# Third place for the decays of a selective scan, in SBUF, and another order in which ScalarE makes them

## What is computed

```python
xp = x @ x_proj_w.T                          # 64 ranks, 16 B columns, 16 C columns
delta = softplus(d_rank @ dt_proj_w.T + dt_proj_b)
deltaA = exp(delta[..., None] * A)           # the decays: rows x channels x 16 states
deltaB_u = delta[..., None] * Bm * x
h = deltaA_t * h + deltaB_u_t                # step by step along the 1024 rows
y = (h * C).sum(states) + x * D
```

## Time and profile before

| what | value |
|---|---|
| median of 3 executions | 4587.7 us (4587.43 to 4588.58) |
| profiled execution, its own time | 4590.48 us |
| its span, first to last instruction | 4588.0 us |
| VectorE (DVE) busy over the span | 3844.8 us, 84% |
| GpSimd (POOL) busy | 3435.0 us, 75% |
| TensorE (PE) busy | 2972.6 us, 65% |
| ScalarE (ACT) busy | 2824.3 us, 62% |
| mean granted TensorE clock | 0.691 of full speed |

### The profile page before, as it was taken

The page is one execution under the profiler, slowest core; times in us unless marked ns, Lnnn a source line. Parts: engine busy times, 40 slices in busy tenths (PEclk is TensorE's granted clock), DMA queues, the critical chain, the costliest instruction groups (busy, mean ns, idle before and its releaser), DMA issues. The chain is left out here.

```text
span 4588.0 us, 60367 instructions
## 1 busy us (share of the span) xinstructions
PE 2972.6 (65%) x17062; PEld 1351.1 (29%) x17062; DVE 3844.8 (84%) x3098; ACT 2824.3 (62%) x4359; POOL 3435.0 (75%) x1748
## 2 busy tenths in 40 slices
PE   3656565656575656566665656565654289999997
PEld 1222222222222222222222222222222145555553
DVE  3999999999999999999999999999998645555542
ACT  5777777777767777777777777777665223232221
POOL 3999999999999999999999999999997100000010
PEclk7667575656565656666575657565655599999998
DMA  4454546364645455454545463646443300000000
GB/s 104 97 135 116 151 105 163 82 167 93 161 102 143 114 136 144 106 140 111 139 115 148 103 159 88 166 93 162 101 126 74 147 13 21 18 18 18 18 19 7
DMA packets 198217, 472.87 MB, mean 103 GB/s; under 512 B 60688, under 2 KB 61200, under 8 KB 197088
## 3 DMA queue, kind: packets, MB, share of 16 engines
q1 hardware_dynamic: 177136, 452.11, 38.9%
q0 software_dynamic: 20736, 16.88, 1.4%
HBM read 126.83 MB, written 73.43 MB: 44 GB/s over the span
## 5 line engine op out<-in xcount | busy, mean ns | idle before, releaser
L882 POOL TENSOR_TENSOR ch<-hid,cmat 128x1024 f32<-128x1024 f32 x1024 | 2391.6, 2362 | 120.3 <-DVE hid L751 102.5
L751 DVE TENSOR_TENSOR_SCAN hid<-decay,inp 128x1024 f32<-128x1024 f32 x1024 | 2270.1, 2268 | 122.6 <-ACT decay L604 122.6
L398 PE MATMUL ps_y<-ch,nsum 128*32 128x256 f32 x8192 | 949.9, 564 | 860.9 <-POOL ch L882 859.2
L604 ACT ACTIVATE decay<-delr,a_neg 128x1024 f32<-128x1024 f32 x1024 | 1133.4, 1113 | 562.1 <-DVE hid L751 550.0
L740 DVE TENSOR_TENSOR inp<-dx,bmat 128x1024 f32<-128x1024 f32 x880 | 1012.6, 1208 | 63.1 <-ACT dx L612 63.1
L398 PEld LDWEIGHTS ps_y<-ch,nsum 128*32 128x32 f32 x8192 | 254.6, 141 | 1527.3 <-POOL ch L882 1313.6
L409 PE MATMUL ps_y<-ident,ysb 128*128 128x128 f32 x1024 | 339.7, 431 | 289.2 <-ACT ysb L619 275.7
L409 PEld LDWEIGHTS ps_y<-ident,ysb 128*128 128x128 f32 x1024 | 246.9, 298 | 524.7 <-ACT ysb L619 484.6
L393 PE MATMUL ps_y<-xhT,dskip 128*32 128x256 f32 x2048 | 260.4, 599 | 217.1 <-ACT xr L626 217.1
L1135 POOL DMA_INDIRECT out_rows<-row,idx_out x16 | 41.1, 2571 | 402.4 <-issue 221.3
L847 POOL TENSOR_TENSOR inp<-dxr,bmat 128x1024 f32<-128x1024 f32 x144 | 340.1, 2362 | 0.0
(11 more groups left out here) (167 smaller groups left out, 3952.7 us busy)
## 6 DMA issues: line engine op xcount, KB each, us to landing
dxr<-dxT SPq DMA_DIRECT2D x1024, 128.0 KB, 2.4
delr<-delT SPq DMA_DIRECT2D x1024, 128.0 KB, 2.4
xr<-in_x SPq DMA_DIRECT2D x32, 1024.0 KB, 6.5
bmat<-b_and_c SPq DMA_DIRECT2D x256, 128.0 KB, 3.4
cmat<-b_and_c SPq DMA_DIRECT2D x256, 128.0 KB, 3.0
x_rows<-xr SPq DMA_DIRECT2D x16, 2048.0 KB, 7.6
out_rows<-xr SPq DMA_DIRECT2D x32, 1024.0 KB, 4.6
w<-in_w SPq DMA_DIRECT2D x2, 4096.0 KB, 24.2
```

What stands on the lines that cost most here:

```text
L398: last = pe.matmul(ps_y[q * CH:(q + 1) * CH, 0:2 * P], nsum[:], ch[:, g, q * 2 * P:(q + 1) * 2 * P], start=False, stop=(g == GROUPS - 1))
L604: nc.scalar.activation(decay[:, g % 2, :], delr[:, c % 2, :], ACT.Exp, scale=a_neg[:, i:i + 1])\
L751: nc.vector.tensor_tensor_scan(hid[:, g, :], decay[:, g % 2, :], inp[:, g, :], 0.0, ALU.mult, ALU.add).then_inc(hid_ready, 1)
L882: nc.gpsimd.tensor_tensor(ch[:, g, :], hid[:, g, :], cmat[:, g, :], ALU.mult).then_inc(ch_ready, 1)
```

## The change

- A third place for decays, `decay2`, an SBUF tensor of 128 x 1024 float32 (4 KB of each partition). The third group (`g == 2`) uses it. The second group has PSUM place 1 to itself; the first and the fourth share PSUM place 0.
- ScalarE makes decays in the order 1, 2, 0, 3 (`DECAYS`). Group 3 of this chunk comes after place 0; group 1 of the next chunk after `copy_dx`, group 2 after place 1, group 0 after place 2. Before the first batch three decays are made, not two.
- The waits follow: group 3 waits for the scan of group 0 of its chunk, group 0 for all scans of the chunk before, groups 1 and 2 for the scan of their own group in the chunk before. `scan` counts `decay_ready` in the new order.
- `copy_dx` and the copies of `y` keep their order among themselves; `copy_dx` now comes ahead of one decay fewer of this chunk.
- `dynamic_dma_scratch_size` goes from 8192 to 4096.

```diff
+DECAYS = (1, 2, 0, 3)
...
+        decay2 = sb("decay2", [P, L])
...
+        def decay_of(g):
+            return decay2[:] if g == 2 else decay[:, int(g == 1), :]
+        def decays(b, c, g):
+            return b * TILES + c * GROUPS + DECAYS.index(g)
...
             def exp_decay(b, c, g):
-                if has(b, 1) or c * GROUPS + g >= 2:
-                    act.wait_ge(hid_ready, tile(b, c, g) - 1)
-                if g == 0:
+                if g == 3:
+                    act.wait_ge(hid_ready, tile(b, c, 0) + 1)
+                elif has(b, 1) or c > 0:
+                    act.wait_ge(hid_ready, tile(b, c, 0) if g == 0 else tile(b, c, g) - GROUPS + 1)
+                if g == DECAYS[0]:
                     act.wait_ge(del_rep[c % 2], (b * (CHUNKS // 2) + c // 2 + 1) * 16 * NT)
                 i = c * GROUPS + g
-                nc.scalar.activation(decay[:, g % 2, :], delr[:, c % 2, :], ACT.Exp, scale=a_neg[:, i:i + 1])\
+                nc.scalar.activation(decay_of(g), delr[:, c % 2, :], ACT.Exp, scale=a_neg[:, i:i + 1])\
                     .then_inc(decay_ready, 1)
...
-                    for g in range(2):
+                    for g in DECAYS[:3]:
                         exp_decay(0, 0, g)
...
                     beside(b, par, c, 0)
-                    exp_decay(b, c, 2)
+                    exp_decay(b, c, 3)
                     if c > 0:
                         copy_y(b, c - 1)
                     elif has(b, 1):
                         copy_y(b - 1, CHUNKS - 1)
-                    exp_decay(b, c, 3)
                     if not (final and c == CHUNKS - 1):
                         copy_dx(*nxt)
+                        exp_decay(*nxt, 1)
...
                     beside(b, par, c, 1)
-                    for g in (0, 1):
-                        if not (final and c == CHUNKS - 1):
-                            exp_decay(*nxt, g)
-                        beside(b, par, c, 2 + g)
+                    if not (final and c == CHUNKS - 1):
+                        exp_decay(*nxt, 2)
+                    beside(b, par, c, 2)
+                    if not (final and c == CHUNKS - 1):
+                        exp_decay(*nxt, 0)
+                    beside(b, par, c, 3)
...
             def scan(b, c, g):
-                dve.wait_ge(decay_ready, tile(b, c, g) + 1)
+                dve.wait_ge(decay_ready, decays(b, c, g) + 1)
...
-                nc.vector.tensor_tensor_scan(hid[:, g, :], decay[:, g % 2, :], inp[:, g, :],
+                nc.vector.tensor_tensor_scan(hid[:, g, :], decay_of(g), inp[:, g, :],
                                              0.0, ALU.mult, ALU.add).then_inc(hid_ready, 1)
...
-    nc = bacc.Bacc("TRN2", target_bir_lowering=False, num_devices=1, dynamic_dma_scratch_size=8192)
+    nc = bacc.Bacc("TRN2", target_bir_lowering=False, num_devices=1, dynamic_dma_scratch_size=4096)
```

## The result

The median of four executions is 4993.64 us (4992.07 to 4995.09) against 4587.97 us before (four executions; the 4587.7 us above are the median of three of them): a ratio of 1.0884, 95% interval 1.0865 to 1.0903. The forecast was 5060 us in a range of 4930 to 5170.

What follows compares the result with a forecast made beforehand. VectorE and GpSimd, both 96% busy, bound the scan stage. From 4588.0 us: +563 blocked products, -102.5 absorbed GpSimd waits, +10 handing over = 5058.5, given as 5060 us, range 4930 to 5170.

Steps and rivals of the forecast that it cites:

- The step that decides: Scan stage: each third-group scan reads two SBUF tensors and blocks GpSimd, 563 us over 256 scans; chance 0.83.
- The estimate by the Trainium skill's rule: Scan stage: the blocking charged at a scan's full length, 256 x 2.27 = 581 us.
- GpSimd's chain would set the end: Scan stage: GpSimd's chain of 3908 us ends the stage, against VectorE's 3328 to 3919 us.
- its waits for scans would be absorbed: Scan stage: GpSimd's 102.5 us of waits for scans vanish, subtracted from the sum.
- the scan itself would not be slower from SBUF: Third group's scans: same duration with both tensors in SBUF; at most 18 us more over 256 scans.
- The charge per scan: GpSimd's loss for each third-group scan: taken as 2.2 us, bounds 2.13 to 2.27, 563 us in all.
- the 10 us for handing over: Scan stage: about 0.04 us per chunk where both VectorE and GpSimd stand, added to the sum as 10 us.
- its own case: The block as summed, chance 0.83: whole-kernel time between 4996 and 5169 us.
- I cost what stays of the waits for decays at nothing: Scan stage: VectorE's 122.6 us of waits for decays taken to vanish; bounds were none or all staying.
- a sign of being wrong: Profile after: the prediction would be wrong if VectorE's waits for decays stayed instead of falling from 122.6 us to near 0.
- 4.6 us of work against 5.6 us of time: First group's decay: ScalarE needs 4.6 us from the third scan's end, and the decay is due after 5.6 us.
- the first rival: Scan stage: the scan blocks nothing, the waits go and GpSimd caps the gain: 4485 us, chance 0.09.

Runs made afterwards that it cites:

- the place alone: The kernel before, in its old order, with the third group's decay in SBUF and the scratch of 4096: 4994.57 us, ratio 1.0889.
- the double dose: The kernel before, old order, scratch 4096, with PSUM place 0 moved to SBUF, so 512 scans have both tensors there: 5502.02 us, ratio 1.1995.

## Why the prediction came out as it did

**What held.** The step that decides, that a scan with both tensors in SBUF shuts GpSimd out, is shown four ways: the changed trace (256 blocked instructions, one for each such scan), the place alone (the whole loss), the double dose (twice the price), and the third group's scan reading PSUM (no loss). The Trainium skill's rule ("SBUF — State Buffer", "Who interferes with whom"), that of a VectorE instruction with two SBUF inputs and a GpSimd instruction that reads SBUF the one issued second is blocked, thus holds for a scan too, in both directions: the scan of 2001.06 waited for GpSimd, and GpSimd for it. The estimate by the Trainium skill's rule, 581 us, was 78 us too high: 503.4 were measured. That GpSimd's chain would set the end, that its waits for scans would be absorbed (99.5 us of its idle time in front of products, forecast 102.5), that the scan itself would not be slower from SBUF (the third group's takes 2.26 us at its shortest, 2.25 before), that the second layer keeps its length and the scratch costs nothing, all came as worked out.

**What was mis-sized.** The charge per scan: 2.2 us, at least 2.13, by the prediction; 503.4 / 256 = 1.97 by the trace. I had let the blocked GpSimd instruction get 0.14 us done meanwhile (it is 0.17: it ends 2.14 us after the scan, where the next one otherwise ends 2.31 after the last), but the waiting scan nothing: issued before its turn, it ends 2.15 us after the product, not 2.27. So a block costs the scan's length less about 0.3 us. That is 563 - 503 = 60 us; the 10 us for handing over didn't show at all, and 3 us less idle time was absorbed. 5058.5 - 60 - 10 + 3 = 4991.5, against a span of 4992.5. The measured 4993.64 us lie 2 us below 4996, the least that the sum allowed inside its own case, and within the range only because that was drawn wider.

**What was wrong, without a price in this sum.** "I cost what stays of the waits for decays at nothing": 76.4 us stayed, hidden because GpSimd set the pace, and 47.1 us with the third place in PSUM. The prediction had itself called that a sign of being wrong. Counted by group, all but 2.9 of the 76.4 us stand before the first group's scan, for which the prediction had set 4.6 us of work against 5.6 us of time. That sum began at the end of the third scan; it left out what ScalarE itself waits for, and the work that this puts off. A wait of ScalarE before the change, the same wait after it, and one late decay after it:

```profile
ACT ysb L619 <- PE ps_y L398: 172.3, 108, 6.4
...
ACT ysb L631 <- PE ps_y L408: 476.5, 159, 8.5
...
2008.43 0.38 ACT L638 ACTIVATE xr<-ps_y 128x256 f32<-128x256 f32 x1 [1.64 <-PE ps_y L420]
...
2012.40 4.47 DVE L765 TENSOR_TENSOR_SCAN hid<-decay,inp 128x1024 f32<-128x1024 f32 x2 [0.31 <-ACT decay L616]
```

ScalarE stood idle 1.64 us for TensorE, and the scan came 0.31 us late. Counted so, ScalarE had waited for TensorE or a DMA, since the first scan of the chunk before, for at least as long as the scan was late in all 63 such cases of the changed kernel, and in 34 of 37 with the third place in PSUM. The traces agree with this reason; no run took these waits away to show it.

So the first rival's price was wrong as well: without the block, the kernel with its third place in PSUM took 4553 us, not 4485. The gain was a third of what the waits promised, since 47 us of them stayed and GpSimd, 8 us behind in busy time, became the one waited for. And a wait I hadn't named appeared: 87.3 us for the fourth group's input, which GpSimd makes; in all 40 cases GpSimd had been shut out while making it.

**Left open.** Whether a GpSimd instruction that doesn't read SBUF would also be shut out wasn't tried. Nor was a third place in PSUM that keeps the whole computation.

## What to carry to other kernels

When VectorE and GpSimd both run without pause, the memory that VectorE's operands lie in is part of the schedule: moving one of two tensors from PSUM to SBUF turned two engines that ran side by side into two that take turns, for about the length of VectorE's instruction each time. Look for a pair of rows, even in another stage, where the same two engines meet with such operands; five copies of 0.18 us that had become up to 0.66 us (the one at 4432.19; the prediction shows one of 0.62) foretold a loss of 406. And where two engines are level within 1%, removing one's waits pays only until the other is waited for: here 75 us of waits removed gave 35.

## What the runs showed of the hardware

A scan with two SBUF tensors that is issued while a GpSimd product of SBUF tensors is under way waits for its end, and the GpSimd instruction behind waits for the scan: so in the chunk shown, and each of the 256 scans held one GpSimd instruction up until 2.13 to 2.16 us after its own end. The price was 1.97 us per scan at 256 scans and 1.92 at 512, or 2.00 for each of the 492 that blocked. With the decay written to SBUF but not read there, the time stayed at that of before (4587.57 us). Both engines' profile durations include the standing still: a GpSimd instruction of 4.35 us and a scan of 4.35 us each did the work of 2.3.
